# Graph network of four layers: the edge attribute product of layer 2 is made in layer 1's edge stage and kept in DRAM

## The reference

```python
# layer 1, edges
messages = relu(x @ W_msg.T + b_msg)
aggregated = segment_sum(messages[src], dst)
# layer 2, edges
msg_in = concatenate([h[src], h[dst], e])          # e: 64 edge attributes
messages = silu(msg_in @ w1 + b1) @ w2 + b2
messages = messages * sigmoid(msg_in @ wg + bg)
agg = segment_sum(messages, dst)
```

## Time and profile before

| | |
|---|---|
| median of 3 runs | 5813.93 us (5810.95 to 5816.22) |
| profiled execution | 5813.95 us, span 5812.3 us |
| mean granted TensorE clock | 0.759 |
| busy: PE, DVE, ACT, POOL | 73%, 57%, 29%, 65% of the span |
| first and last gather of layer 1's edge stage | 2030.5 and 3078.8 us |
| first and last gather of layer 2's edge stage | 3194.4 and 4568.8 us |
| bytes moved by DMA | 442.03 MB |

### The profile page before, as it was taken

How to read it: one execution, slowest core, us unless ns; L and a number is a source line. 1 busy time by engine, 2 the same in 40 slices (tenths; PEclk the granted TensorE clock), 3 DMA queues, 4 the chain that set the end, 5 groups by cost and what they waited for, 6 DMA issues and landing times. The chain is left out here.

```text
span 5812.3 us, 106638 instructions
## 1 busy us (share of the span) xinstructions
PE 4224.1 (73%) x20886; PEld 3052.0 (53%) x20887; DVE 3311.8 (57%) x10595; ACT 1685.6 (29%) x5074; POOL 3782.6 (65%) x3395
## 2 busy tenths in 40 slices
PE   0178878788874334444447999999999868888888
PEld 0156666666663333333335677777777645555555
DVE  4265655555553633333336555555555568888886
ACT  0132222222221000000002333333333445555554
POOL 2178888888886077777771665555655257777774
PEclk9865555555555655555557999999999989999999
DMA  5755555555555211111111333333333123333332
GB/s 140 217 77 70 70 71 70 70 70 70 71 70 97 58 51 52 52 52 52 52 52 57 108 98 98 98 99 98 99 97 99 46 60 58 58 57 57 57 57 54
DMA packets 741221, 442.03 MB, mean 76 GB/s; under 512 B 434953, under 2 KB 675443, under 8 KB 740602
## 3 DMA queue, kind: packets, MB, share of 16 engines
q0 software_dynamic: 217824, 319.22, 26.8%
q1 hardware_dynamic: 523322, 121.99, 10.6%
HBM read 355.73 MB, written 116.63 MB: 81 GB/s over the span
## 5 line engine op out<-in xcount | busy, mean ns | idle before, releaser
L632 POOL DMA_INDIRECT G<-table,src_it x2496 | 2415.7, 968 | 1196.1 <-issue 694.0
L608 POOL DMA_INDIRECT sums<-work,idx x832 | 1295.8, 1557 | 282.8 <-issue 186.3
L1295 DVE TENSOR_TENSOR big<-bank,big 128x129 f32 (+2 forms) x2496 | 886.3, 355 | 930.8 <-PE bank L710 512.1
L710 PE MATMUL bank<-G,oh 128*128 128x129 f32 x1664 | 428.6, 439 | 628.9 <-DMA G<-table,src_it 628.9
L744 PE MATMUL bank<-work 128*128 128x128 f32 x1664 | 621.5, 475 | 212.6 <-DVE work L1342 185.9
L710 PEld LDWEIGHTS bank<-G,oh 128*128 128x128 f32 x1664 | 372.7, 329 | 684.7 <-issue 479.8
L849 PE MATMUL bank<-big,oh 128*128 128x320 f32 x1664 | 592.8, 461 | 110.9 <-DVE big L1295 110.7
L955 ACT ACTIVATE work<-bank,work 128x128 f32<-128x128 f32 x832 | 306.2, 368 | 1082.0 <-PE bank L736 1082.0
L744 PEld LDWEIGHTS bank<-work 128*128 128x128 f32 x1664 | 406.5, 303 | 402.6 <-DVE work L1342 399.7
L736 PE MATMUL bank<-big,work 128*128 x1664 | 577.0, 449 | 0.1
L1282 DVE TENSOR_TENSOR oh<-iota,rel_it 128x512 f32<-128x512 f32 x625 | 428.6, 686 | 157.2 <-issue 88.2
(11 more groups left out here) (226 smaller groups left out, 6382.8 us busy)
## 6 DMA issues: line engine op xcount, KB each, us to landing
G<-e_src SPq DMA_DIRECT2D x832, 64.0 KB, 3.1
G<-table,src_it POOLq DMA_INDIRECT x2496, 2.5
work<-e_a SPq DMA_DIRECT2D x832, 32.0 KB
e_a<-in_edge_attr_dram POOLq DMA_DIRECT2D x1, 25000.0 KB, 102.0
sums<-work,idx POOLq DMA_INDIRECT x832
work<-e_a SPq DMA_DIRECT2D x832, 4.0 KB
work<-e_a SPq DMA_DIRECT2D x832, 2.0 KB
sums<-big POOLq DMA_DIRECT2D x4, 3264.0 KB
```

The lines of the kernel that those rows point to most:

```text
L608: pool.indirect_dma_start(sums[k % COPIES], bass.IndirectOffsetOnAxis(ap=idx[:, k:k + 1], axis=0), z_out[:, k, :], None, compute_op=ALU.ad ...
L632: pool.indirect_dma_start(G[:, k, 0:wid], None, tab, bass.IndirectOffsetOnAxis(ap=src_it[:, n:n + 1], axis=0)).then_inc(quad_in[layer - 1] ...
L710: mm = t.matmul(bank[4 * o + j][:, 0:wid], oh[:, n, :], G[:, n, 0:wid], start=True, stop=True)
L1295: v.tensor_tensor(to, ps, to, ALU.add).then_inc(EDGE[layer]["acc_done"], 1)
```

## The change

The product of the 64 edge attributes is taken out of layer 2's edge stage. In layer 1's edge stage SP loads the attributes, TensorE transposes them and makes the product (banks 4, 5 and 6; layer 1's aggregation now uses banks 0 to 3, two items in each), ScalarE copies it to `E1`, and SP writes 512 KB a round to a DRAM tensor `e_pre`. In layer 2's edge stage SP reads 512 KB a round back into `E2`, two rounds deep. DVE adds the gathered rows to it in place, one operation of 1,024 columns whose inputs and output all lie in SBUF; this operation's semaphore `eg_done` now frees the slots of `G`. The add of PSUM (L1393 before) takes `E2` in place of `G`. The four accumulations on DVE no longer stand in one row but between the other operations.

```diff
+        e_pre = dram("e_pre", [QUADS + 4, P, 4, 256])
...
+            def edge_products():                       # SP, layer 1
...
+                    if live(0):
+                        if live(2):
+                            held(sp, ph["t_done"], q - 1)
+                        for j in range(4):
+                            r = sp.snap(regs[k % 4 * 4 + j], min_val=0, max_val=ROWS - 1)
+                            sp.dma_start(a64[:, k % 2 * 4 + j, :], e_a64[bass.ds(r * P, P), :]).then_inc(attr2[k % 2], 16)
                     if live(2):
+                        held(sp, ph["e_ready"], q - 1)
+                        sp.dma_start(e_pre[...], E1[...]).then_inc(e_out[k % 2], 16)
+                quad_steps(sp, 2, top, body, 4)
+                for k in range(2):
+                    sp.wait_ge(e_out[k], 16 * (QUADS // 2))
+
+            def load_products():                       # SP, layer 2
...
+                    if live(2):
+                        held(sp, ph["add_done"], q - 1)
+                    sp.dma_start(E2[...], e_pre[...]).then_inc(e_back[k % 2], 16)
...
-                freed = EDGE[layer][(None, "agg_done", "add_done", "prod_done")[layer]]
+                freed = EDGE[layer][(None, "agg_done", "eg_done", "prod_done")[layer]]
...
# TensorE, layer 1
+                    if live(1):
+                        pe.wait_ge(ph["ev_done"], q)
+                        if live(2):
+                            pe.wait_ge(ph["e_ready"], q - 1)
+                        for j in range(4):
+                            h = 64 * (j % 2)
+                            mm = t.matmul(bank[5 + j % 2][:, j // 2 * 256:j // 2 * 256 + 256], eT1[h:h + 64, (k - 1) % 2, j // 2, :],
+                                          We2[h:h + 64, :], start=True, stop=True)
+                        mm.then_inc(ph["e_done"], 1)
+                    if live(0):
+                        pe.wait_ge(attr2[k % 2], landed(64, 2, q, k, 0))
+                        if live(1):
+                            pe.wait_ge(ph["ev_done"], q)
+                        for j in range(2):
+                            mm = t.transpose(bank[4][:, j * P:(j + 1) * P],
+                                             a64[:, k % 2 * 4 + 2 * j:k % 2 * 4 + 2 * j + 2, :].rearrange("p a f -> p (a f)"), ident[:])
+                        mm.then_inc(ph["t_done"], 1)
                     if live(1):                        # the aggregation, as before
...
# ScalarE, layer 1
+                    if live(0):
+                        act.wait_ge(ph["t_done"], q + 1)
...
+                        a.activation(eT1[...], bank[4][:, 0:256], ACT.Copy).then_inc(ph["ev_done"], 1)
+                    if live(1):
+                        act.wait_ge(ph["e_done"], q)
+                        if live(3):
+                            act.wait_ge(e_out[o], landed(16, 2, q, k, 3))
+                        for h in range(2):
+                            last = a.activation(E1[:, o, h::2, :], bank[5 + h][:, :]..., ACT.Copy)
+                        last.then_inc(ph["e_ready"], 1)
...
# layer 2: TensorE keeps L765, L779, L788, L798, L800, L807; L770 and L790 go; ScalarE's L982 goes
# DVE, layer 2
+                    def with_products(q, k):
+                        dve.wait_ge(e_back[k % 2], landed(16, 2, q, k, 0))
+                        dve.wait_ge(quad_in[1][k % 4], landed(64, 4, q, k, 0))
+                        to = E2[:, k % 2, :, :].rearrange("p j f -> p (j f)")
+                        v.tensor_tensor(to, to, G[:, k % 4 * 4:k % 4 * 4 + 4, :].rearrange("p j f -> p (j f)"),
+                                        ALU.add).then_inc(ph["eg_done"], 1)
...
# order in an iteration: add(0); L1393 of q-1, with E2 for G; add(1); with_products(q);
# add(2); message of q-2; add(3); one-hots of q+1
```

More of the change, by code:

```diff
@@ L128, in gnn_layers @@
         pre2, sg2 = view(0, [4, 256]), view(1024, [2, 4, 128])
[L129 to L132, removed]
+        sil2, silT2, msg2 = view(2048, [4, 128]), view(2560, [4, 128]), view(3072, [2, 4, 128])
+        ohT2 = view(4096, [256]).bitcast(BF16).rearrange("p (a b) -> p a b", b=128)
+        E2 = view(4992, [2, 4, 256])
+        a64, eT1, E1 = view(0, [8, 64]), view(512, [2, 2, P]), view(1024, [2, 4, 256])
         spare3 = big[:, NBT * L3W:BIGW]
@@ L193, in gnn_layers @@
         quad_in = [[sem(f"quad_in{layer}_{k}") for k in range(4)] for layer in (1, 2, 3)]
-        attr3 = [sem(f"attr3_{k}") for k in range(8)]
+        e_out, e_back = [sem(f"e_out{k}") for k in range(2)], [sem(f"e_back{k}") for k in range(2)]
+        attr3, ATTR3_BEFORE = attr_in[0:8], 16 * (ITEMS // RING)
         fc_zero, fc_in, fc_ready = sem("fc_zero"), sem("fc_in"), sem("fc_ready")
@@ L762, in body @@
                             b = pe.snap(regs[k % 4 * 4 + j], min_val=0, max_val=NB)
-                            to = bank[1 + j % 2][:, j // 2 * 256:j // 2 * 256 + 256]
                             for piece in range(3):
[L765 to L771, removed]
+                                mm = t.matmul(bank[1 + j // 2][:, j % 2 * 256:j % 2 * 256 + 256], ohT2[:, j, :],
+                                              Qp[:, bass.ds(b, 1), piece * 256:(piece + 1) * 256].rearrange("p o f -> p (o f)"),
+                                              start=(piece == 0), stop=(piece == 2))
                         mm.then_inc(ph["pre_done"], 1)
@@ L787, in body @@
                         for j in range(4):
[L788 to L791, removed]
+                            mm = t.transpose(bank[0][:, j * P:(j + 1) * P], oh[:, k % 4 * 4 + j, :], ident[:])
                         mm.then_inc(ph["t_done"], 1)
@@ L1378, in body, with add @@
                 def body(q, k, live):
+                    def add(j):
+                        add_item(2, regs[k % 4 * 4 + j], bank[6 + k % 2][:, j * P:(j + 1) * P],
+                                 4 * q - 16 + j if live(5) or j else None)
+                    def with_products(q, k):
[4 more added lines that the diff above has]
+                                        ALU.add).then_inc(ph["eg_done"], 1)
                     if live(4):
                         dve.wait_ge(ph["agg_done"], q - 3)
-                        for j in range(4):
-                            add_item(2, regs[k % 4 * 4 + j], bank[6 + k % 2][:, j * P:(j + 1) * P],
-                                     4 * q - 16 + j if live(5) or j else None)
+                        add(0)
                     if isinstance(q, int) and q == 0:
@@ L1386, in body @@
                     if live(1):
[L1387 removed]
                         dve.wait_ge(ph["pre_done"], q)
[L1389 removed]
+                        dve.wait_ge(ph["eg_done"], q)
                         if live(2):
@@ L1403, in body @@
                                                op0=ALU.add, op1=ALU.mult).then_inc(ph["msg_done"], 1)
+                    if live(4):
+                        add(3)
                     if live(0) and not (isinstance(q, int) and q == QUADS - 1):
```

57 lines of the change are left out of this document (34 added, 23 removed).

## The result

| | before | after |
|---|---|---|
| median | 5815.07 us | 5593.61 us (5593.06 to 5595.21, 4 runs) |
| ratio | 1 | 0.9621, 95% interval 0.9604 to 0.9638 |
| span of the profiled execution | 5812.3 us | 5593.6 us |

The account below looks back on a forecast made before the run. GpSimd, its gathers held by DVE, was to bound layer 2 at 5.02 + 0.29 + 0.44 = 5.75 us a round. Layer 2's -193, layer 1's +31 and the ends' +13 gave -149: 5665 us, range 5550 to 5800.

Parts of the forecast that it names:

- L: Layer 2: time from the start of a round's last gather until its rows can be used, taken as 2.95 us.
- The first hold: Layer 2: the new add, still running 0.12 us into a gather (its point), holds that gather for 0.29 us a round.
- second hold: Layer 2: the one-hot comparison behind the new add holds the fourth gather for 0.44 us a round.
- The read of E2: Layer 2: the 512 KB read each round costs between 2.1 and 4.2 us and stays hidden within about 7.1.
- Layer 1: Edge stage: TensorE's added work and the later comparison cost 0.15 us a round together, +31 us.
- TensorE on the edge of 5.03: Layer 1: at half clock TensorE's work takes 4.99 us, or about 4.7, beside four gathers of 5.03 us.
- Ends: Last write after layer 1 must land before the barrier, +5 us; layer 2's last round drains behind its last gather, +8.
- Rival 1: Layer 2: the adds don't hold gathers further, so TensorE's 5.29 us a round bounds it; 5569 us, chance 0.12.
- Rival 2: Layer 2: gathers land just before 2.62 us or near 3.8, round 6.60, layer 1 costs 62 us; 5872 us, chance 0.13.
- Rival 3: Layer 1: TensorE bounds it at half clock, 5.7 us a round, +135 us in place of 31; 5769 us, chance 0.12.
- Rival 4: Layer 2: the E2 read is late, each us beyond 7.1 costing 104 us; two make about 5870 us, chance 0.03.
- Rival 5: Layer 2: the new add also waits for a gather under way, on average 0.35 us, +73; 5738 us, chance 0.05.

Follow-up runs that it names:

- H3: Changed kernel, but layer 2's new add takes a PSUM bank in place of E2 and its one-hot comparison reads columns from PSUM: 5508.48 us, ratio 0.9481 to before.
- E4: Changed kernel, but layer 2 reads 64 KB of the products a round in place of 512 KB: 6763.73 us against 6669.71 before, ratio 1.0140.
- G1: The changed kernel itself, unedited, run again on another chip as a control: 6755.27 us against 6666.96 for the kernel before, ratio 1.0132.
- second set: Three runs on one chip: the kernel before, 5811.42 us; the changed kernel without layer 1's edge product, 5576.05; and H3, 5508.48.
- F3: Changed kernel with all four of layer 2's accumulations on DVE ahead of the new add: 6600.27 us against 6598.04 before, ratio 0.9999.

## Why the prediction was right, and where its sizes were off

**What bounds layer 2 after.** Right, and shown: H3 took the holds away and the rounds followed. GpSimd is the bound through gathers held by two DVE operations, one of them new. Gathers wait for nothing, DVE waits for the gather before the new add, TensorE is at 90% (the text said under 90), and two gathers in four are long, one by each operation.

**The size of it.** Forecast 5.75, measured 5.54 us a round. Two terms were too large. L was taken as 2.95 us; after shows 4009.41 - 4006.24 - 0.34 = 2.83. The first hold was then 0.19 in place of 0.29. In the second hold L cancels, because the add's end shifts the next point and the comparison alike. It is set by DVE's chain from the add's start to the comparison's, which took 2.14 us, not 2.21, and by small differences in the two operations' lengths: 0.34 in place of 0.44. The two differences are 0.20 us a round, 42 us. The add itself took 1.22 us (forecast 1.21). The step of L that I over-sized is the surcharge for rows of twice the bytes and for the 512 KB read, 0.4 us together; it was 0.29, and how this divides between rows and read was not measured. Both errors go the same way; nothing in the forecast offset them.

**The read of E2.** Right that it is hidden: it landed in 3.8 us at the median (3.4 to 4.1), inside the 2.1 to 4.2 given, and of the 128.1 us for which DVE stood before the new add from 3300 to 4200 us, 125.1 were for the gather. E4, with an eighth of the bytes, has the ratio of G1 (1.0140 and 1.0132), but on chips where gathers didn't set the pace, and on two different ones, so it adds little.

**Layer 1.** Right in kind, half in size: +0.08 us a round in place of 0.15, by the windows 16 us in place of 31. The cause is the comparison that now falls later against the gathers, one of the two named. The other, TensorE on the edge of 5.03, did not come: by the forecast's 4.7 us of work it would have been some 90% busy at half clock (an estimate), and by the mean of 0.78 it got full clock in about half of the time.

**Ends.** The +5 after layer 1 and +8 after layer 2 were not there. From layer 2's first gather to layer 3's first the time fell by 235.2 us, and the rounds account for (6.68 - 5.54) x 208 = 237, so the end costs 2. After layer 1 the stretch even became 2.9 us shorter: the last write is no wait that counts. So the 70 us between the forecast difference of 149 and the spans' 218.7 are made up like this: layer 2's rounds 44 (237 - 193), its end 6 (8 - 2), layer 1 with its end 24 (36 forecast, 11.9 measured from its first gather to layer 2's), less 4.6 for the rest of the table above, which was forecast at nothing.

**The rivals.** Rival 1 (no hold) is what H3 made real, and it would have been faster than forecast: its floor of 5.29 was itself too high by 0.2 at least. Rival 2 (the add ends later or earlier, round 6.60) did not come. Its lower edge was not at L = 2.62, as forecast, but lower, at about 2.46 (see below), 0.37 us from the measured 2.83; and just under 2.62 the hold by the forecast's own terms would have been 1.21, not 1.14. Rival 3 did not come: the clock rose to a mean of 0.78. Rival 4 did not either. Rival 5, a new add that waits for gathers under way, falls too, as the next line shows. What nobody forecast, neither a rival nor I, is the chip on which the same change costs 1.3%.

All 208 adds of after, with their minimum, median and maximum in ns:

```profile
L1434 DVE TENSOR_TENSOR work<-work,G x208: 1224/1225/1227, 3216.6 to 4365.1; 128x1024 f32<-128x1024 f32 x104
```

They spread over 3 ns, though gathers were under way at the start of many: no add of after was stretched.

There is a small exclusion in the other direction all the same, which the prediction did not have. The 14 traces hold 108 one-hot comparisons with both inputs in SBUF that started between 0.05 us before and 0.03 us after a gather's start and took 0.70 to 0.77 us, in place of 0.68 to 0.69. Every one of the 108 ended 0.72 us after the gather's start, and the gather kept its 0.94 to 0.96. The 29 comparisons with one input in PSUM that started in the same stretch took 0.693 us at most. One of the 108, in layer 1 of after:

```profile
2606.60 0.77 DVE L1329 TENSOR_TENSOR oh<-iota,rel_it 128x512 f32<-128x512 f32 x1
2606.64 0.94 POOL L654 DMA_INDIRECT G<-table,src_it  x1 [0.30 <-issue]
```

So what decides is which of the two starts first. A comparison or new add with two SBUF inputs that starts 0.05 us or more ahead of the gather holds it, and the gather ends 0.82 us after the operation does; that is why only what is left 0.12 us into the gather counts. One that starts 0.03 us before the gather or later never held it, though it ran across the point at 0.12 us: in some 2,100 such pairs no gather lost more than 0.013 us. Where the two start almost together, the DVE operation is delayed instead, by 0.09 us at most. The prediction's rule, that the point must fall inside the operation, is right for operations already running when the gather starts, as nearly all those of layer 2 are. The size of the loss is not a share of time but a matter of phase: a gather that is caught pays all that is left of the operation.

## What to carry to other kernels

When an engine's loop is shortened, ask who sets the pace next, and count what the new operation does to that one: here 112 us of held gathers, 44 of which were there before, stand beside a gain of 221. A DVE operation with both inputs in SBUF holds an indirect DMA that GpSimd begins while it runs (204 comparisons of 0.68 us cost 70 us in layer 2 of after); one input in PSUM ends that at no cost in DVE's own time (1.21 us in H3, 1.22 in after), and a hold can be found in a trace by laying each long gather beside what DVE runs at that moment. Where a forecast turns on how such patterns fall, follow one round on one time axis with the measured distances and keep the distance to the next jump as the bound (0.37 us here).

## What the runs showed of the hardware that was not expected

- **The same kernels take 13 to 15% longer on some chips.** The kernel before took 5812 to 5815 us in the first runs and on the chip of the second set, and 6598, 6667 and 6670 us on three others. Each of these chips was used for one set of runs only, so chip and hour can't be told apart. In the slower runs layer 0 takes what it always did (layer 1's first gather starts at 2029.5 us in G1 and at 2033.3 in after). The three edge stages with loops written out by hand are slower, with engines that stand without a cause in the trace. On SP the trace of F3 has some 420 intervals of 0.69 to 0.76 us between starts of instructions over 600 gathers of layer 1, and some 550 of layer 3; after has 3 and 0. That instructions arrive late would fit this. It is a guess that no experiment tested, and why these chips differ stays open.
- **On such a chip the change loses 1.3%** (G1, 1.0102 to 1.0162). Where it loses is not shown. If layer 1 of before took its 5.05 us there too, it lost 0.92 x 208 = 191 us there with the change, and layer 2 must have won about 100 for the sum to be +88; if layer 1 was slow before as well, layer 2 won less or nothing. No trace of before was taken on such a chip, so this split is argued only.
- **The clock of TensorE alternates by rounds** in layer 1: the same products (eight instructions) took 1.13 us in one round (granted clock 1.00) and 2.08 in the next (0.50), at a mean of 0.78 and 69% busy. Before the change, at 41% busy, the mean was 0.50.
